# First attention's queries and keys as two fp32r halves in 48 rows per head, two heads to an fp32 transpose, in place of six bf16 parts in 96 rows

## What is computed

```python
N, L, _ = x.shape
q = (x @ Wq.T).reshape(N, L, H, D).transpose(0, 2, 1, 3)      # H = 16, D = 16
k = (x @ Wk.T).reshape(N, L, H, D).transpose(0, 2, 1, 3)
v = (x @ Wv.T).reshape(N, L, H, D).transpose(0, 2, 1, 3)
q = _layernorm(q, gq, bq)
k = _layernorm(k, gk, bk)
scores = jnp.einsum('nhld,nhmd->nhlm', q, k)
scores = jnp.where(causal, scores, NEG)
attn = jax.nn.softmax(scores, axis=-1)
out = jnp.einsum('nhlm,nhmd->nhld', attn, v)
return out.transpose(0, 2, 1, 3).reshape(N, L, EMB) @ Wo.T + bo
```

## Time and profile before

| what | value |
|---|---|
| three runs | 4105.27, 4112.76 (median), 4118.48 us |
| profiled execution | span 4099.4 us from first to last instruction; the page gives no other time of its own |
| median less span | 13.4 us |
| PE busy | 3512.7 us (86%) |
| weight loads busy | 2772.0 us (68%) |
| DVE busy | 3056.1 us (75%) |
| ACT busy | 2303.1 us (56%) |
| POOL busy | 776.0 us (19%) |
| one batch, stage 1 to 3 | 1339.6 to 1372.7 us, 33.1 us |
| the same batch, attention 1 to its last split | 1372.7 to 1429.2 us, 56.5 us |

### The profile page before, as it was taken

One profiled execution on the slowest core, in us unless ns is written; L12 is line 12 of the kernel. 1 busy time (PEld: TensorE's weight loads), 2 busy tenths in 40 slices (PEclk: granted clock), 3 DMA queues, 4 the chain that ended last, 5 costly groups with the idle time before them and its releaser, 6 DMA issues.

```text
span 4099.4 us, 93010 instructions
## 1 busy us (share of the span) xinstructions
PE 3512.7 (86%) x31392; PEld 2772.0 (68%) x31392; DVE 3056.1 (75%) x6444; ACT 2303.1 (56%) x6346; POOL 776.0 (19%) x919
## 2 busy tenths in 40 slices
PE   3898988989889898898988889888898988989888
PEld 2676766767667676676766767666676766767667
DVE  3878777787777877768787787877778777787776
ACT  2656546565465664646655465654656546565464
POOL 1212222022120221212122121222202212022120
PEclk9999999999899999999999999998999989999899
DMA  3000000000000000000000000000000000000000
GB/s 73 7 2 7 7 7 7 2 7 7 7 7 1 8 6 7 7 7 7 2 7 7 7 7 2 7 7 7 7 2 7 7 7 7 2 7 7 6 1 6
DMA packets 33906, 30.35 MB, mean 7 GB/s; under 512 B 8864, under 2 KB 33312, under 8 KB 33376
## 3 DMA queue, kind: packets, MB, share of 16 engines
q1 hardware_dynamic: 33376, 23.68, 2.0%
HBM read 15.28 MB, written 8.39 MB: 6 GB/s over the span
## 4 chain that ended last, share of the span: by engine, by line
PE 56%; issue 14%; DVE 13%; ACT 10%; POOL 5%; SPq 1%; ACTq 0%; DMA 0%; DVEq 0%; POOLq 0%
PE bank L619 12%; PE scores L717 9%; ACT prob L833 6%; PE bank L630 6%; PE scores L606 6%; PE bank L729 5%; PE scores L607 4%; PE scores L608 3%; POOL qf L499 2%; PE scores L691 2%; PE scores L671 2%; PE scores L602 2%; PE bank L590 2%; DVE negmax L1049 1%; DVE stk L1145 1%
## 5 line engine op out<-in xcount | busy, mean ns | idle before, releaser
L833 ACT ACTIVATE prob<-scores,negmax 128x128 f32<-128x128 f32 (+3 forms) x2048 | 1060.8, 538 | 223.6 <-DVE negmax L1049 180.2
L1049 DVE TENSOR_REDUCE negmax<-scores 128x1 f32<-128x128 f32 (+3 forms) x2048 | 884.5, 483 | 102.0 <-PE scores L608 88.4
L619 PE MATMUL bank<-ident,prob 128*128 128x128 f32 x5120 | 731.2, 280 | 44.5 <-DVE probt L1057 35.1
L1057 DVE COPY probt<-bank 128x512 f32<-128x512 f32 x896 | 596.6, 683 | 180.1 <-PE bank L619 173.1
L619 PEld LDWEIGHTS bank<-ident,prob 128*128 128x128 f32 x5120 | 548.6, 142 | 155.5 <-DVE probt L1057 65.9
L606 PE MATMUL scores<-khh,qt 128*128 128x256 f32 (+2 forms) x1024 | 439.2, 430 | 13.3 <-issue 6.6
L608 PE MATMUL scores<-mask,ident 128*128 128x128 bf16 x2048 | 450.4, 231 | 0.0
L833 ACT ACTIVATION_READ_ACCUMULATOR prob<-scores,negmax 128x1 f32 x2048 | 438.0, 214 | 0.0
L804 ACT ACTIVATE probt<-bank 128x512 f32<-128x512 f32 x384 | 233.0, 607 | 205.3 <-PE bank L619 205.3
L607 PE MATMUL scores<-kll,qt 128*128 128x256 f32 (+2 forms) x1024 | 346.1, 338 | 0.0
L590 PE MATMUL bank<-ident,stk 128*96 128x128 bf16 x2048 | 206.9, 288 | 149.8 <-DVE stk L1147 119.7
(11 more groups left out here) (178 smaller groups left out, 6937.0 us busy)
## 6 DMA issues: line engine op xcount, KB each, us to landing
x_in<-in_x_rows SPq DMA_DIRECT2D x16, 512.0 KB, 3.5
out_rows<-x SPq DMA_DIRECT2D x16, 512.0 KB, 3.5
r_gu<-in_wg SPq DMA_DIRECT2D x2, 512.0 KB, 5.1
r_gu<-in_wu SPq DMA_DIRECT2D x2, 512.0 KB, 5.1
r_d<-in_wd SPq DMA_DIRECT2D x1, 1024.0 KB, 6.5
r_wqt<-in_wq_nope_t SPq DMA_DIRECT2D x1, 512.0 KB, 6.8
r_wqr<-in_wq SPq DMA_DIRECT2D x2, 256.0 KB, 8.6
r_wob<-in_wo SPq DMA_DIRECT2D x1, 512.0 KB, 5.3
```

What stands on the lines that cost most here:

```text
L619: ins = nc.tensor.transpose(bank[4 + n % 2][:, q * P:(q + 1) * P], prob[:, u % 2, q, i * P:(i + 1) * P], ident[:, :])
L833: nc.scalar.activation(prob[:, u % 2, q, 0:n], bank[q][:, 0:n], ACT.Exp, bias=negmax[:, a, u, q:q + 1], accum_out=sums[:, a, u, q:q + 1]). ...
L1049: nc.vector.tensor_reduce(negmax[:, a, u, M * part:M * part + M], scores[:, M * part:M * part + M, 0:n], axis=AX.X, op=ALU.max, negate=Tru ...
L1057: nc.vector.tensor_copy(probt[:, u % 2, i], bank[4 + n % 2][:, :]).then_inc(probt_dve.sem, 1)
```

## The change

Queries and keys of the first attention are kept as two parts in fp32r instead of six slots of bf16. Each head has four slots of 16 channels: queries are high, low, high; keys are high, high, low; the fourth slot is padding that only fills 64 columns. Two heads then fill 128 columns, and one fp32 transpose with the fp32 identity turns both. Head h lies in rows 0 to 47 or 64 to 111 of qkt, and the score is one fp32r matmul over 48 rows. Its moving side is at least 256 columns wide (m), so a 128-wide unit computes twice its columns; the surplus is not read.

ACT fills the high slots in two copies, DVE the low slots in two subtractions from the normalised tile; the buffer res1 is gone. POOL sets the padding to zero twice per batch, after the adds to x_in. DVE waits, before it overwrites a normalised tile, until its own subtractions of two tiles earlier are complete. PE waits for the padding at tiles 0 and 1. In the diff, a line in brackets names engine and function.

```diff
-SPLITS = 6
-SD = SPLITS * D
+SLOTS = 4
+HW_ROWS = SLOTS * D
+USED = 3 * D
...
-    qkt = new("qkt", [SD, 2 * H, L], BF16)
+    qkt = new("qkt", [P, H, L], F32R)
...
-    res1 = at("res1", [P, 2, 2 * C], F32, o + 8192)
-    stk = at("stk", [P, 2, 2 * H, SPLITS, D], BF16, o + 12288)
+    stk = at("stk", [P, 2, 2 * H, SLOTS, D], F32R, o + 8192)
...
-    part1_ready = Signal(sem("part1_ready"), NT)
+    pad_ready = Signal(sem("pad_ready"), 2)
+    high_ready = Signal(sem("high_ready"), NT)
...
-    DVE_LINKS, POOL_LINKS, ACT_LINKS = 28, 18, 4
+    DVE_LINKS, POOL_LINKS, ACT_LINKS = 20, 18, 4
...
 (POOL, sequence)
             for t in range(NT):
                 nc.gpsimd.tensor_tensor(x_in[:, t], x_in[:, t], bo[:, :], ALU.add).then_inc(xb_ready.sem, 1)
+            for s in range(2):
+                nc.gpsimd.memset(stk[:, s, :, 3].bitcast(F32), 0.0).then_inc(pad_ready.sem, 1)
...
 (PE, transpose_stack)
             pe.wait_ge(stack_ready.sem, stack_ready.at(b, t + 1))
+            if t < 2:
+                pe.wait_ge(pad_ready.sem, pad_ready.at(b, t + 1))
...
-                out = bank[4 + quad].bitcast(BF16)
-                for i in range(8):
-                    ins = nc.tensor.transpose(out[0:SD, i * P:(i + 1) * P],
-                                              stk[:, t % 2, quad * 8 + i].rearrange("p s d -> p (s d)"), ident16[:, :])
+                for i in range(4):
+                    h = quad * 8 + 2 * i
+                    ins = nc.tensor.transpose(bank[4 + quad][:, i * P:(i + 1) * P],
+                                              stk[:, t % 2, h:h + 2].rearrange("p h s d -> p (h s d)").bitcast(F32), ident[:, :])
...
 (PE, score)
+                m = max(n, 2 * P)
                 if a == 0:
-                    mm(bank[q][:, 0:n], qkt[:, h, j * P:(j + 1) * P], qkt[:, H + h, 0:n], start=True, stop=False)
+                    rows = slice(h % 2 * HW_ROWS, h % 2 * HW_ROWS + USED)
+                    mm(bank[q][:, 0:m], qkt[rows, h // 2, j * P:(j + 1) * P], qkt[rows, (H + h) // 2, 0:m], start=True, stop=False)
...
 (ACT, copy_stack; DVE's has the same change for quads 1 and 3)
-                copy(qkt[:, quad * 8:(quad + 1) * 8, t * P:(t + 1) * P],
-                     bank[4 + quad].bitcast(BF16)[0:SD].rearrange("p (h t) -> p h t", h=8)).then_inc(stackt_act.sem, 1)
+                copy(qkt[:, quad * 4:(quad + 1) * 4, t * P:(t + 1) * P],
+                     bank[4 + quad].rearrange("p (h t) -> p h t", h=4)).then_inc(stackt_act.sem, 1)
...
 (ACT, sequence)
-                    copy(stk[:, s, 0:H, 0:3], qv.to_broadcast([P, H, 3, D]))
-                    copy(stk[:, s, H:2 * H, 0:4:3], kv.to_broadcast([P, H, 2, D]))
-                    copy(stk[:, s, H:2 * H, 5], kv[:, :, 0]).then_inc(part1_ready.sem, 1)
+                    copy(stk[:, s, 0:H, 0:3:2], qv.to_broadcast([P, H, 2, D]))
+                    copy(stk[:, s, H:2 * H, 0:2], kv.to_broadcast([P, H, 2, D])).then_inc(high_ready.sem, 1)
...
 (DVE, sequence)
                     dve.wait_ge(rq_ready.sem, rq_ready.at(b, t + 1))
+                    if t >= 2:
+                        dve.wait_ge(stack_ready.sem, stack_ready.at(b, t - 1))
...
-                    dve.wait_ge(part1_ready.sem, part1_ready.at(b, t + 1))
-                    rv = res1[:, s].rearrange("p (h d) -> p h d", d=D)
-                    chain.link(tt(rv, qn[:, s].rearrange("p (h d) -> p h d", d=D), stk[:, s, :, 0], ALU.subtract))
-                    nc.vector.tensor_copy(stk[:, s, 0:H, 3:5], rv[:, 0:H].unsqueeze(2).to_broadcast([P, H, 2, D]))
-                    chain.link(nc.vector.tensor_copy(stk[:, s, H:2 * H, 1:5:3], rv[:, H:2 * H].unsqueeze(2).to_broadcast([P, H, 2, D])))
-                    tt(stk[:, s, 0:H, 5], rv[:, 0:H], stk[:, s, 0:H, 3], ALU.subtract)
-                    tt(stk[:, s, H:2 * H, 2], rv[:, H:2 * H], stk[:, s, H:2 * H, 1], ALU.subtract).then_inc(stack_ready.sem, 1)
+                    dve.wait_ge(high_ready.sem, high_ready.at(b, t + 1))
+                    v = qn[:, s].rearrange("p (h d) -> p h d", d=D)
+                    tt(stk[:, s, 0:H, 1], v[:, 0:H], stk[:, s, 0:H, 0].bitcast(F32), ALU.subtract)
+                    tt(stk[:, s, H:2 * H, 2], v[:, H:2 * H], stk[:, s, H:2 * H, 0].bitcast(F32), ALU.subtract).then_inc(stack_ready.sem, 1)
```

More of the change, by code:

```diff
@@ L600, in score @@
                     pe.wait_ge(prob_ready.sem, prob_ready.at(b, (a * UNITS + u - 1) * G + q + 1))
+                m = max(n, 2 * P)
                 if a == 0:
-                    mm(bank[q][:, 0:n], qkt[:, h, j * P:(j + 1) * P], qkt[:, H + h, 0:n], start=True, stop=False)
+                    rows = slice(h % 2 * HW_ROWS, h % 2 * HW_ROWS + USED)
+                    mm(bank[q][:, 0:m], qkt[rows, h // 2, j * P:(j + 1) * P], qkt[rows, (H + h) // 2, 0:m], start=True, stop=False)
                 else:
-                    m = max(n, 2 * P)
                     tok = qt[:, h, j * P:(j + 1) * P]
@@ L1036, in copy_stack @@
                 dve.wait_ge(stackt_psum.sem, stackt_psum.at(b, 4 * t + quad + 1))
-                nc.vector.tensor_copy(qkt[:, quad * 8:(quad + 1) * 8, t * P:(t + 1) * P],
-                                      bank[4 + quad].bitcast(BF16)[0:SD].rearrange("p (h t) -> p h t", h=8)).then_inc(stackt_dve.sem, 1)
+                nc.vector.tensor_copy(qkt[:, quad * 4:(quad + 1) * 4, t * P:(t + 1) * P],
+                                      bank[4 + quad].rearrange("p (h t) -> p h t", h=4)).then_inc(stackt_dve.sem, 1)
         def copy_q(b, n):
```

## The result

The changed kernel is slower: 4345.88 us (median of 4 runs, 4344.51 to 4348.36) against 4113.32 us for the kernel before beside it (4 runs), a ratio of 1.0567 with the 95% interval 1.0552 to 1.0581. The prediction was 4079 us, with a range from 4042 to 4126. Over 16 batches the medians make it 14.5 us more per batch where 2.1 less was forecast; the two profiled executions are 15.4 apart.

What follows compares the result with a forecast made beforehand. Bound: before attention 1 a chain over four tiles, no engine always busy; in attention 1, PE alternating with ACT's exponentials. Gain 4.6 less loss 2.5 is 2.1 us per batch, 34 over 16: 4079 us, range 4042 to 4126.

Steps and rivals of the forecast that it cites:

- (a): Before attention 1: DVE's per-tile work becomes two subtractions, so it is on time at POOL's scale; 1.7 us gained per batch.
- POOL keeps the pace: Rival, before attention 1: POOL's multiply and add fill what DVE gives up, (a) gains nothing; 4106 us, chance 0.12.
- (b): Before attention 1: ACT's three fills of 1.67 us become two copies of at most 1.23; 0.5 us gained.
- (c): Before attention 1: DVE, with less to copy, starts on time when ACT ends; 0.4 us gained.
- (d): Before attention 1: DVE's start to PE's first transpose falls from 2.39 us to 0.85 to 0.9; 1.5 us gained.
- (e): Last tile before attention 1: first transpose to first score takes 2.8 us instead of 3.35; 0.5 gained, 1.0 lost at low clock.
- the added columns: Attention 1: 128-wide units compute 256 columns; this cost alone was the lower bound of the loss, 0.6 us per batch.
- The 5.9 us of the upper bound: Attention 1: all of PE's extra time per batch on the path, where the forecast took a loss of 2.5 us.
- Cold start: Rival: shorter transpose work leaves PE's clock low when attention 1 begins, 8 heads costing 2.4 us; 4142 us, chance 0.14.
- Attention has no room: Rival, attention 1: all of PE's extra 5.9 us is paid, 1.3 us later per batch; 4134 us, chance 0.05.
- Weights hidden: Rival, attention 1: the 48-row fp32r weight load hides behind the mask, loss only 0.6 us; 4049 us, chance 0.12.
- attention grows by over 4 us: Sign that the forecast is wrong: attention 1 growing beyond 4 us, where 56.5 us was expected to become about 59.

Runs made afterwards that it cites:

- a_rows128: The changed kernel with each score matmul of attention 1 over all 128 rows instead of 48, summing two heads' products: 4040.81 us, 0.985 of the kernel before.
- b: The changed kernel with attention 1's mask matmul over only the 64 rows of the head's half, half of each mask left out: 4074.94 us, 0.9924 of the kernel before.
- f1b: The changed kernel with padding moved to each head's first slot, even heads over 80 rows, odd over the upper 64: 4137.48 us, 1.007 of the kernel before.

## Why the prediction was wrong

**The stage before attention 1 was right in its sum**: forecast 4.6 us earlier, measured 5.4 (33.23 to 27.86). The timeline of its last tiles, all engines, after:

```profile
1436.88 0.25 POOL L486 TENSOR_TENSOR rq<-rq 128x32 f32<-128x32 f32 x1
...
1437.17 0.69 DVE L1136 TENSOR_TENSOR qn<-scores,rq 128x512 f32<-128x512 f32 x1 [1.24 <-POOL rq L486]
...
1440.85 1.15 ACT L810 ACTIVATE stk<-qn 128x512 fp32r<-128x512 f32 x2 [2.42 <-POOL qn L493]
...
1442.03 0.42 DVE L1150 TENSOR_TENSOR stk<-qn,stk 128x256 fp32r<-128x256 f32 x1 [1.23 <-ACT stk L810]
...
1442.92 2.06 PE L595 MATMUL bank<-ident,stk 128*128 128x128 f32 x16 [1.14 <-DVE stk L1151]
...
1445.85 0.35 PE L609 MATMUL scores<-qkt 48*128 48x256 f32 x1 [0.88 <-DVE qkt L1042]
```

- (a) DVE is on time at POOL's scale: 0.04 us behind its end at 1437.13, not 0.6. From the first projection to ACT's copies it is 22.85 us in this batch, before 25.33: 2.5 less, forecast 1.7. So "POOL keeps the pace" did not happen.
- (b) ACT's copies 1.15 us, forecast at most 1.23, before 1.67.
- (c) DVE starts 0.03 us after them, forecast on time.
- (d) 0.89 us to the first transpose, forecast 0.85 to 0.9, before 2.39.
- (e) 2.93 us from first transpose to first score, forecast 2.8, and at full clock.

From ACT's copies to the first score the gain is 2.8 us, forecast 2.9. So the excess lies in what (a) covers; what in it is not attributed further.

Two bounds of the sum do not follow from the terms shown: with 0.5 in place of 0.25 in (a) the stage's upper bound is 5.1 and not 5.3, and the added columns alone are 16 heads of 0.05 us, 0.8 before any slack and not 0.6. Neither moves the forecast.

**The failed step is the price of a head in attention 1.** The prediction took "0.25 for one fp32r matmul of 256 columns and a mask" from attention 2. Types and columns were the same there, but both of those matmuls are over 128 rows, and the new one is over 48. The runs put 0.48 in its place, and a_rows128 shows that 0.25 was right for 128 rows. The 5.9 us of the upper bound counted only columns and weights, so the bound was wrong too, and with it the range. Low clock in attention 1 stood in the sum at nothing; only the rival "Cold start" had it, at 2.4 us. Before the change the kernel had 96 against 128 rows, on one side of the border, so no row of its trace showed the price in attention 1.

By the starts, against a_rows128: 32 heads of 256 columns cost 0.23 us more, 16 of 384 cost 0.07 more (0.53 against 0.46, for ACT was the wait there), 16 of 512 cost 0.22 more. That is 7.4 + 1.1 + 3.5 = 12 us of the 19.4 between 77.8 and 58.4. The remaining 7 us I put down to the low clock, as the rest; it was not measured alone. Of it, the 14 heads a batch that ran at 0.50 account for 4.2 us by their medians (0.73, 0.83 and 0.94 us against 0.47, 0.53 and 0.58).

The Trainium skill, "TensorEngine Tiling (Array Packing)", section "Tiling Modes", says that changing the tiling mode, as against changing tiles within one, drains the engine. The runs agree on both, if the border between 64 and 80 rows is a change of mode: 0.10 to 0.12 us a change across it, and no such price between halves (b). The prediction did not weigh it.

**The rivals.** "Attention has no room" had the right place, but with 5.9 us little more than a quarter of the 21.2 that came. "Weights hidden" did not come: the load of 48 rows takes 0.205 us on average, where 128 took 0.209, and at a change it starts only with its own product. The group of weight loads after:

```profile
L609 PEld LDWEIGHTS scores<-qkt 48*128 48x128 f32 x1024 | 210.3, 205 | 124.9 <-issue 34.6 <-ACT qkt L810 17.3 <-ACT prob L839 12.9
```

"Cold start" named low clock as the danger, and 0.14 was its chance. But attention began at full clock, and the reason given (shorter transposes) was not it, as a_rows128 has the same transposes and 0.2 us of low clock. The cost is a part of the growth rather than all of it. The clock fell to 0.50 at 1434.96 and rose to 1.00 at 1438.37, and between 1433.85 and 1439.73 PE did nothing but fp32 transposes. The Trainium skill, "TensorE: Matmul & The Clock Gate", section "Part 4: PE-mode transpose", says that transposes do not count as activity for the clock; this rise does not agree, and the measurement decides. The two timeline rows of PE:

```profile
1434.98 3.60 PE L595 MATMUL bank<-ident,stk 128*128 128x128 f32 x16 [0.48 <-DVE stk L1151]
...
1439.73 2.05 PE L595 MATMUL bank<-ident,stk 128*128 128x128 f32 x16 [1.15 <-DVE stk L1151]
```

Of the prediction's own tests, "attention grows by over 4 us" caught it, and so did heads at 0.48 us where 0.25 should show.

## What to carry to other kernels

Before a matmul is made to use fewer rows, look at what stands beside it on PE. A price read from matmuls of the same type and width does not carry over if one neighbour has at most 64 rows and the other more (here 80, 96 or 128). That costs 0.10 to 0.12 us each way, twice per head, so together nearly as much as the head's own 0.25 us. Zero rows that lift the count above 64 took no time of their own (f1b: 0.21 us from product to mask over 80 rows, as over 128). And an order that groups like with like saves changes, but pays with the engine that waited for the first result.

## What the runs showed beyond that

- The price of a change does not double at half the clock. In bf16 a head of 256 columns at 0.50 took 0.547 us over 64 rows and 0.349 over 80 (these are medians of starts in the traces, here of 7 and 6): 0.10 a change, as at full clock (0.374 and 0.170). In fp32r a pair of heads of 384 columns at 0.50 took 1.67 us with four changes (the changed kernel) and 1.40 with two (f1b): 0.14 a change, and 0.11 at full clock (1.06 and 0.84).
- PE's clock fell in the middle of uninterrupted work and stayed low through it: 23.00 us busy out of 23.00 at 0.50, in the third windows row at the top.
- The second subtraction of DVE, which began while POOL was multiplying, took 1.49 us instead of 0.42, in three tiles of four and in every batch. The first, which in the same tiles began ahead of POOL's multiply and overlapped it too, kept its 0.42. The timeline of DVE and POOL after, the third tile and the fourth:

```profile
1437.94 1.37 POOL L492 TENSOR_TENSOR qn<-qn,gam 128x512 f32<-128x512 f32 x1 [0.81 <-DVE qn L1136]
1438.11 1.49 DVE L1151 TENSOR_TENSOR stk<-qn,stk 128x256 fp32r<-128x256 f32 x1
...
1442.37 0.42 DVE L1151 TENSOR_TENSOR stk<-qn,stk 128x256 fp32r<-128x256 f32 x1
```

It seems to have cost little here, since the last tile's chain waits for POOL (ACT's copies [2.42 <-POOL qn L493] above); that was not tested. The Trainium skill, "GPSIMD Engine Reference", section "1. Specifications", names contention between POOL and DVE instructions with two SBUF inputs; both subtractions have two, and the trace agrees for the second.
